# A first pass by single PSUM banks, maxima ahead of the turned tokens, and another opening and end, in a one-core attention and feed-forward kernel

## The reference

```python
xn = layernorm(x)                                   # last axis, 256
q = (xn @ wq + bq).reshape(b, s, 16, 16)            # 16 heads of 16
k = (xn @ wk + bk).reshape(b, s, 2, 16)             # 2 groups of keys and values
v = (xn @ wv + bv).reshape(b, s, 2, 16)
q, k = rotary(q) * 16 ** -0.5, rotary(k)
attn = softmax(q @ k.T * 16 ** -0.5)                # 1024 x 1024 for each batch and head
a = (attn @ v) @ wo + bo
hidden = silu(xn @ W1.T) * (xn @ W3.T)              # 1024 wide
f = fwht(hidden) @ W2.T                             # Walsh-Hadamard transform, scaled
return x + a + f
```

## Time and profile before

| what | us |
|---|---|
| median of three runs | 1079.11 (1078.23 to 1080.97) |
| the profiled execution, whole | 1075.6 |
| its span | 1073.8 |
| PE busy | 1014.3 |
| DVE busy | 771.2 |
| ACT busy | 707.5 |
| POOL busy | 347.2 |
| DVE's reductions of the first pass, L1295, 512 of them | 619.0 |
| DVE idle just before them | 235.7 |

### The profile page before, as it was taken

The page is one execution under the profiler, slowest core; times in us unless marked ns, Lnnn a source line. Parts: engine busy times, 40 slices in busy tenths (PEclk is TensorE's granted clock), DMA queues, the critical chain, the costliest instruction groups (busy, mean ns, idle before and its releaser), DMA issues.

```text
span 1073.8 us, 19578 instructions
## 1 busy us (share of the span) xinstructions
PE 1014.3 (94%) x7604; PEld 549.6 (51%) x7604; DVE 771.2 (72%) x934; ACT 707.5 (66%) x1336; POOL 347.2 (32%) x300
## 2 busy tenths in 40 slices
PE   4889999999999999999999999999999999999997
PEld 3554445545554555545554455545555454644454
DVE  5996688677776778767786777767776778776723
ACT  4256677657765777657776577667775678566873
POOL 5262722073312634054310735126320224012300
PEclk9998999999999999999999999999999999999999
DMA  8762155212052253402242250521123131510001
GB/s 234 177 172 75 53 137 104 74 57 86 17 117 78 76 136 66 100 21 84 64 103 74 97 126 18 117 64 51 51 62 71 33 83 33 111 32 6 12 8 50
DMA packets 64941, 84.03 MB, mean 78 GB/s; under 512 B 19960, under 2 KB 34168, under 8 KB 64848
## 3 DMA queue, kind: packets, MB, share of 16 engines
q1 hardware_dynamic: 63296, 80.74, 29.1%
q10 hardware_dynamic: 1552, 2.03, 0.7%
HBM read 54.97 MB, written 22.51 MB: 72 GB/s over the span
## 4 chain that ended last, share of the span: by engine, by line
PE 66%; DVE 17%; ACT 5%; issue 4%; DMA 4%; SPq 3%; POOL 2%; DVEq 0%; ACTq 0%; POOLq 0%
PE ps L1501 16%; PE ps L1558 14%; PE ps L1545 13%; DVE negpart L1295 11%; PE ps L1456 9%; PE ps L1513 8%; PE ps L1467 3%; DVE hid L1267 3%; PE ps L1434 3%; ACT work L1079 2%; DMA qk_parts<-hid 1%; DMA xn<-in_x 1%; SPq L776 1%; SPq L784 1%; DMA recip_rows<-dens 1%
## 5 line engine op out<-in xcount | busy, mean ns | idle before, releaser
L1295 DVE TENSOR_REDUCE negpart<-ps 128x2 f32<-128x1024 f32 x512 | 619.0, 1224 | 235.7 <-PE ps L1456 234.8
L1079 ACT ACTIVATE work<-ps 128x512 f32<-128x512 f32 x1024 | 560.0, 603 | 262.3 <-PE ps L1545 256.9
L1558 PE MATMUL ps<-work,vb 128*32 128x512 f32 x2048 | 274.6, 609 | 5.8 <-ACT osum L1090 5.0
L1545 PE MATMUL ps<-qh,kb 50*128 50x512 f32 x1024 | 265.1, 450 | 10.3 <-ACT work L1079 7.4
L1456 PE MATMUL ps<-kb,qh 48*128 48x512 f32 x1024 | 226.8, 433 | 9.6 <-DVE negpart L1295 5.3
L1545 PEld LDWEIGHTS ps<-qh,kb 50*128 50x128 f32 x1024 | 123.4, 185 | 212.3 <-ACT work L1079 159.0
L1501 PE MATMUL ps<-xf,w_p 64*128 64x512 f32 x1536 | 218.3, 400 | 7.4 <-DVE negpart L1295 1.4
L1501 PEld LDWEIGHTS ps<-xf,w_p 64*128 64x128 f32 x1536 | 143.6, 185 | 49.7 <-DVE hid L1267 16.3
L933 POOL TENSOR_TENSOR hid_p<-hid,hid_p 128x512 fp32r<-128x512 f32 x64 | 82.2, 1286 | 203.1 <-ACT hid_p L1068 203.1
L1456 PEld LDWEIGHTS ps<-kb,qh 48*128 48x128 f32 x1024 | 98.1, 185 | 82.7 <-DVE negpart L1295 48.4
L1513 PEld LDWEIGHTS ps<-w2t_p,hid_p 64*128 64x128 f32 x1536 | 107.7, 185 | 34.2 <-DVE negpart L1295 27.1
(11 more groups left out here) (125 smaller groups left out, 484.6 us busy)
## 6 DMA issues: line engine op xcount, KB each, us to landing
xf<-xn_parts SPq DMA_DIRECT2D x32, 512.0 KB, 8.5
qh<-qk_parts SPq DMA_DIRECT2D x192, 64.0 KB, 2.3
xn_parts<-xt SPq DMA_DIRECT2D x14, 512.0 KB, 3.5
qh<-mturned SPq DMA_DIRECT2D x256, 2.0 KB
y<-in_x SPq DMA_DIRECT2D x8, 512.0 KB, 4.8
attnt<-osum SPq DMA_DIRECT2D x124, 32.0 KB, 2.0
recips<-recip_rows SPq DMA_DIRECT2D x120, 32.0 KB, 1.8
xn<-in_x SPq DMA_DIRECT2D x7, 512.0 KB, 5.0
```

The lines of the kernel that those rows point to most:

```text
L1079: nc.scalar.activation(prob[(ITSTEPS * i + j) % NPROB][:, h, :], ps[:, 4 + u % 3, :], ACT.Exp, scale=SCALE).then_inc(exp_done, 1)
L1295: nc.vector.tensor_reduce(negpart[a][:, f, :, h, t, e], two(slot), AX.X, ALU.max, negate=True).then_inc(ring_free[slot], 1)
L1545: pe.matmul(ps[:, 4 + u % 3, :], kb[i % 2][rows, kt * P:(kt + 1) * P], qh[2 * a + f][rows, h, :], start=True, stop=True).then_inc(s2_done, 1)
L1558: m = pe.matmul(ps[VW * h:VW * (h + 1), 7, :], vb[b % 2][g][:, kt, :], prob[(ITSTEPS * i + j) % NPROB][:, h, :], start=(kt == 0), stop=(kt ...
```

## The change

- The first pass goes by single banks. `first(slot, 0)` issues the unit's half on the upper 64 rows into the slot's second bank, `first(slot, 1)` the other half into the first bank, and PE's order puts other work between them. DVE reduces each bank by itself: 1024 reductions of 128x512 instead of 512 of 128x1024. A half waits only for its own bank (the fourth field of `RING`), where the slot's last work was a unit too.
- PE's order in every kind of period is written anew, and in ACT's the place of `gate`, `linear`, `save_sums` and the projections' copies. WOo takes WO's order.
- SP: `place_maxima` and the reciprocals go ahead of `load_turned`.
- Opening: the first queries are copied from the rotated tiles straight into `qh` (`first_queries`, 24 transfers on SP's and ACT's queues), the turned tokens go from `xt` to `xf` (`copy_turned`); of the ten operations that rotate the second block's queries DVE keeps five, ACT has two and POOL three. EARLY is 3, so one UP piece more lies in iteration 0, in place of a period without own work.
- End: DN of iteration 7 begins a period earlier, the first half of the last WO is in its last period; the last sums are turned, divided and turned back on DVE, from PSUM, and multiplied with `wo_last`, a copy of the weights with zero rows.

The diff, cut to its core:

```diff
-EARLY = 4
-LATER = (4, 6, 8, 10)
-BEGIN = 8
+EARLY = 3
+LATER = (4, 6, 7, 8, 10)
+BEGIN = 12
 W2ALL = 32
-W2HEAD = 24
+W2HEAD = 20
...
+def down_at(i):
+
+    return range(12, 16) if i + 1 < NIT else range(11, 15)
...
+    if i + 1 == NIT and p == PERIODS - 1:
+        return ("WO", i, 0)
+    if p in down_at(i):
+        return ("DN", i, down_at(i).index(p))
...
-    def first(slot):
+    def first(slot, *halves):
         nonlocal unit
-        at = i + unit // (2 * UNITS)
-        if at < NIT:
-            piece(("S1", at, unit // UNITS % 2, unit % UNITS), 0, slot)
-        unit += 1
+        for n in halves:
+            at = i + unit // (2 * UNITS)
+            if at < NIT:
+                piece(("S1", at, unit // UNITS % 2, unit % UNITS), n, slot)
+            unit += n
...
         if kind in ("UP", "UPo"):
-            own(0, 1)
-            first(1)
+            own(0)
+            first(1, 0)
+            own(1)
+            first(1, 1)
             scores(0)
             sums_before()
+            first(1, 0)
             scores(1)
-            first(1)
-            own(2)
+            first(1, 1)
+            own(2, 3)
+            first(1, 0)
             scores(2)
-            own(3)
-            first(1)
+            first(1, 1)
             sums(i, 2 * p)
             scores(3)
-            first(1)
+            first(1, 0, 1)
...
+        elif kind in ("WO", "WOo"):
+            first(1, 0)
+            scores(0)
+            first(1, 1)
+            scores(1)
+            first(1, 0)
+            scores(2)
+            first(1, 1)
+            own(0, 1, 2, 3)
+            scores(3)
+            first(1, 0, 1)
+            sums_before()
+            first(0, 0, 1)
+            sums(i, 2 * p)
...
-def walk_closing(sums, piece, select):
+def walk_closing(sums, piece, last_values):
     sums(NIT - 1, ITSTEPS - 1)
-    select()
-    for half in range(QB):
-        for k in range(4):
-            piece(("WO", NIT - 1, half), k, 1 - half)
+    last_values()
...
+            at[entry] = (slot, full[slot], free[slot], free[slot] - (entry[0] == before[slot] == "S1"))
+            before[slot] = entry[0]
...
+            if m == 1:
+                return
...
+        def first_queries(queue, parts):
+
+
+            for part, n in parts:
+                queue.wait_ge(*rq(0, (6, 8, 9, 10)[part]))
+                for r in range(ROWT):
+                    for h in range(PAIRS):
+                        to = GRP * r + HD * n + HD // 2 * (part // 2)
+                        queue.dma_start(qh[0][to:to + HD // 2, h, :].bitcast(F32),
+                                        turning(0)[0][(0, 2, 3, 1)[part]][ROWT * h + r:P:NH, :]).then_inc(q_in[0], 16)
...
+            def copy_turned():
+
+                sp.wait_ge(*freed(("XT", 0)))
+                for n in range(2):
+                    for r in range(ROWT):
+                        for c in range(ROWT):
+                            sp.dma_start(xf[n][GRP * r:GRP * (r + 1), c:KC:ROWT, :].bitcast(F32),
+                                         xt[n][GRP * c:GRP * (c + 1), :, :].bitcast(F32)).then_inc(xf_in, 16)
...
-            store_turned(0)
             store_keys(sp, 0)
             swap_keys(1)
+            first_queries(sp, ((0, 0), (0, 2), (2, 0)))
+            store_keys(sp, 1)
+            copy_turned()
+            store_queries(1)
+            load_queries(0, 0, 1)
             store_queries(0)
-            store_keys(sp, 1)
-            load_queries(0, 0, 0)
-            load_turned(0)
-            store_queries(1)
             load_x(2)
-            load_queries(0, 0, 1)
+            place_maxima(0, 0, 0)
+            store_turned(1)
+            load_queries(0, 1, 0)
...
-                if after:
-                    load_turned(i + 1)
-                    load_queries(i + 1, 1, 0)
                 spread_recips(i, 0)
                 if after:
                     place_maxima(i + 1, 0, 0)
+                    load_queries(i + 1, 1, 0)
+                    load_turned(i + 1)
                     load_queries(i + 1, 1, 1)
...
+            a, b, t, u = turning(1)[0]
+            pool.wait_ge(*rq(1, RQ1))
+            nc.gpsimd.tensor_tensor(b, b, u, ALU.add).then_inc(q1_sum, 1)
+            pool.wait_ge(q1_hi, 1)
+            nc.gpsimd.tensor_tensor(t.bitcast(F32R), t, a, ALU.subtract).then_inc(q1_lo, 1)
+            pool.wait_ge(q1_hi, 2)
+            nc.gpsimd.tensor_tensor(b.bitcast(F32R), b, u, ALU.subtract).then_inc(q1_lo, 1)
...
+                for n, r in enumerate((1, 0)):
+                    dve.wait_ge(*filled(("S1", i, a, u), n + 1))
+                    nc.vector.tensor_reduce(negpart[a][:, f, r, h, t, e:e + 1], two(slot)[:, r, :], AX.X, ALU.max,
+                                            negate=True).then_inc(ring_free[slot], 1)
...
+                if k == 0 and RING[entry][3] > 0:
+                    pe.wait_ge(ring_free[slot], RING[entry][3])
+                if k == 1 and RING[entry][2] > RING[entry][3]:
...
+                    r = ROWT - 1 - k
+                    rows = slice(GRP * r, GRP * r + SROWS)
+                    m = pe.matmul(bank[:, r, :], qh[2 * q + f][rows, h, t * P:(t + 1) * P],
+                                  kb[i % 2][rows, e * 512:(e + 1) * 512], start=True, stop=True)
+                    done = True
...
+            def last_values():
+
+
+                pe.wait_ge(norm_done, 2 * NIT)
+                for k in range(BT):
+                    bank = ps[:, 2 + k, 0:D]
+                    pe.matmul(bank, attnt[0:GRP, 1, k * P:(k + 1) * P], wo_sb[0:GRP, NG - 1, :], start=True, stop=False)
+                pe.wait_ge(wo_last_in, 16 * QUAD)
+                for k in range(BT):
+                    pe.wait_ge(last_norm, k // 2 + 1)
+                    bank = ps[:, 2 + k, 0:D]
+                    m = pe.matmul(bank, last_attn[:, k * P:(k + 1) * P], wo_last, start=False, stop=True)
+                    if k % 2 == 1:
+                        m.then_inc(last_full, 1)
...
                     if kind == "UP":
                         exponentials(i, j, 0, 4)
                         hidden_before(i, p)
+                        gate(i, up_at(i).index(p))
                         exponentials(i, j, 4, 5)
-                        gate(i, up_at(i).index(p))
-                        exponentials(i, j, 5, 6)
                         linear(i, up_at(i).index(p))
-                        exponentials(i, j, 6, 8)
...
+            dve.wait_ge(pv_done, ITSTEPS * NIT)
+            for n, cols in enumerate(halves):
+                nc.vector.transpose(last_sums[:, cols], ps[:, 7, cols]).then_inc(last_turned, 1)
             for n in range(2):
-                cols = slice(n * 2 * P, (n + 1) * 2 * P)
-                dve.wait_ge(last_turned, 1)
-                nc.vector.reciprocal(last[GRP:P, cols], ps[GRP:P, 5, cols]).then_inc(last_recip, 1)
-                dve.wait_ge(last_turned, 2)
-                dve.wait_ge(last_recip, n + 2)
-                nc.vector.tensor_tensor(attnt[GRP:P, 1, cols], ps[GRP:P, 4, cols], last[GRP:P, cols],
-                                        ALU.mult).then_inc(last_norm, 1)
-            projected_sums(NIT - 1, 0)
+                dve.wait_ge(last_turned, n + 1)
+                nc.vector.reciprocal(shares[n], blocks[n][:, :, HD]).then_inc(last_step, 1)
             for n in range(2):
-                at = y[:, (NBLK - 1) % 2, 2 * n:2 * n + 2, :].rearrange("p t d -> p (t d)")
-                dve.wait_ge(*filled(("WO", NIT - 1, 1), n + 1))
-                nc.vector.tensor_tensor(at, at, two(0)[:, n, :], ALU.add).then_inc(ring_free[0], 1)
+                dve.wait_ge(last_step, n + 1)
```

More of the change, by code:

```diff
@@ L250, in walk_iteration @@
             scores(0)
-            first(1)
+            first(0, 0, 1)
+            first(1, 0)
             scores(1)
-            sums_before()
-            scores(2)
-            first(1)
-            own(0, 1)
-            sums(i, 2 * p)
-            first(1)
-            scores(3)
-            own(2, 3)
-            first(1)
-            extra()
-        elif kind == "WOo":
-            first(0)
+            first(1, 1)
+            scores(2)
+            own(0, 1, 2)
+            first(1, 0)
```

423 lines of the change are left out of this document (221 added, 202 removed).

## The result

The changed kernel takes 1063.61 us (median of four, 1059.54 to 1072.10) where the kernel before, run beside it, takes 1078.67: a ratio of 0.9853, 95% interval 0.9820 to 0.9886. A second measurement gave 0.9844 (0.9811 to 0.9877). So it is faster, by 15 us and not by the 44.5 forecast, and stands 1.6 above the range. The profiled execution took 1059.54 (span 1057.7).

The account below looks back on a forecast made before the run. PE and DVE were taken to wait for each other over both banks of slot 1. Terms -10 -9 -15 -10 +3 +3 -2.5 -4 sum to -44.5: 1031 from the profiled 1075.6, 1034.5 as median; range 1013 to 1062.

Parts of the forecast that it names:

- UP: UP periods in the loop: 7.4 us for 7.59, a gain of 10 in all (ends 0 and 29).
- DN: DN periods in the loop, 31 of them: 7.2 us against 7.45 on average, a gain of 9 (ends 0 and 14).
- Broken pairs: Rival, first pass: 543 same-row neighbours at 0.1 us each cost 54, kernel slower by 9 (1088 us); chance 0.07.
- Turning periods: Five stretches of 33.6 us: half units between score pairs fill PE's waits for ACT, 3.0 each, 15 gained (0 to 25).
- WOo: Four periods of about 11.3 us: WO's order, with copy and sums placed later, gains 2.5 each, 10 (0 to 14).
- Tokens: Iterations 6 and 7: turned tokens, issued later on SP's queue, come 0 to 5 us late twice, costing 3 (0 to 10).
- SP's queue otherwise: Maxima on SP's queue some 5 us earlier: no old stall to win back, though the shorter iteration would have met one.
- Opening: Opening: copies inside SBUF, first unit near 41, less lead, added UP piece and smoother start; 2.5 us gained in all.
- A smoother start: Opening: PE ran at 1.2 GHz from 78 to 89 after a wait; a smoother start wins 3 of about 5 us.
- End: Tail after the last sums' start: 9.2 us becomes 1.0 + 4.7, a gain of 4 (ends 0 and 5).
- DVE's load: DVE's 1024 short reductions: busy 703 us instead of 619, 84 more, on an engine judged not full.
- periods without own work: Seven periods left, near DVE's pace: eight short reductions cost 4.8 us for 4.6, 0.4 each with waits, +3.

Follow-up runs that it names:

- adjacent: Changed kernel with both halves of a unit issued together at the place of the second, banks still reduced singly: 1100.92 us, 1.0165 of the kernel before.
- lean_qk: Changed kernel with two instead of three matmuls per product in the projections of blocks 2 to 7: 1068.18 us, 0.9861 of the kernel before.
- tokens_undo: Changed kernel with SP's old order in every iteration, tokens and queries ahead of reciprocals and maxima: 1092.39 us, 1.0094 of the kernel before.
- before_gap: Kernel before with W2HEAD 20 instead of 24 and without the wait pacing the head of the weights' product: 1088.84 us, 1.0074 of the kernel before.
- head28: Changed kernel with W2HEAD 28 instead of 20, more of the weights' product ahead of the first unit: 1055.73 us, 0.9756 of the kernel before.
- best1: Changed kernel with W2HEAD 28 and, for iterations 6 and 7, tokens ahead of reciprocals and maxima: 1053.70 us, 0.9767 of the kernel before.
- best2: best1 with the second block's keys stored ahead of SP's last query copies and loaded on SP's queue, not ACT's: 1049.23 us, 0.9715 of the kernel before.

## Why the prediction was wrong, point by point

- **UP, -10 forecast**: right. 7.39 by the chain above, which has the product in it; 0.20 x 59 = 11.8.
- **DN, -9**: right, 7.22 for 7.2 forecast.
- **Broken pairs, the slower rival**: did not happen (adjacent).
- **Turning periods, -15**: the step's size failed. The four periods that took 33.6 take 32.4 now (33.2 in iteration 1): some 1.2 each and 5.8 in all. PE in time, their first matmul and the one behind them:

```profile
444.77 0.50 PE L1544 MATMUL ps<-kb,qh 48*128 48x512 f32 x1
...
477.13 0.86 PE L1587 MATMUL ps<-xf,w_p 64*128 64x512 f32 x6
```

  "PE's floor by the prices above is about 27.5" took pair prices from UP. Counted from one start to the next over this stretch, a score matmul takes 0.207 and a first-pass one 0.174, where a pair at 0.235 would be 0.118 each: 30.3 without a gap, and 2.1 of gaps. And lean_qk shows that less issue would have become waits for ACT, DVE and POOL.
- **WOo, -10**: mis-sized. From own(0) of the UP before to own(0) of the one behind is 16.4 for 17.2 in iteration 6 and for 18.8 in iteration 7: 0.7 and 2.4, of which 0.2 is the UP's. "Some 11.3" was the length of one of them; the other was 9.6. Those at period 0 took 9.3 up to UP's own(0) and take 8.3 if the wait for tokens is taken off: 1.0 each. That is 4.7 in all.
- **Tokens, +3**: the mechanism right, the size wrong. Waits of 3.37 and 4.18, in the two places named, and the clock behind them; iteration 7 with the end shows 6.0 between late (128.3) and in time (122.3), and with the 3.4 of iteration 6 that is some 9.5.
- **SP's queue otherwise, at nothing**: the new place of the maxima is worth 28.5 by tokens_undo. The prediction had seen that "the shorter iteration would have met one"; it did not price the clock behind such waits.
- **Opening, -2.5**: the step that failed worst. Up to the first score the sum held -2 (3 won at the first unit, 1 lost in the lead; its other two terms lie behind that score), and +10.1 came. "First unit near 41" rested on issues of 0.45; the copies took 0.76 each on SP and 0.84 for most on ACT, so that twelve on either queue took 9.2 and 9.3 and not 5.4, and the unit started at 43.54 for 43.61. The head shortened from 24 to 20 was not priced; with the queries no earlier, it made a wait of 3.86. "A smoother start would win some of about 5, I take 3" did not come: behind the first score the clock is at 0.50 again from 84 to 88 and from 96 to 100, and in the whole execution 18.6 us more of clock are lost, most of it ahead of the first score. before_gap (+8.3) and head28 (-7.9) put a price on the short head from both sides.
- **End, -4**: right. From the last sums' start to the last addition's end is 5.8 (1049.22 to 1055.04), for 9.8.
- **DVE's load**, in the argument and not in the sum: "84 more" busy time was forecast and 35.6 came. Reductions in a row overlap, 1024 of 685 ns being busy 659.1 and not 701. They still have 512 elements each, so the advice on tile size that the prediction sets against the edit is kept.

The books: the profiled execution is 16.1 shorter where the sum said 44.5, 28.4 missing. For the opening and iteration 0 the sum held 2.8 of gain (2.5 for the opening, 1.8 for UP and DN, less 1.5 for periods without own work), and 7.8 of loss came: 10.6 missing. For iterations 1 to 5 it held 27.6 (6.8 for UP, 5.8 for DN, 15 for turning), and 20.0 came: 7.6 missing, the turning periods' 9.2 less what UP did better. For iterations 6 and 7 with the end it held 14.2 (2.4 for UP, 2.3 for DN, 10 for WOo and 4 for the end, less 3 for tokens and some 1.5 for periods without own work), and 4.0 came: 10.2 missing, of which WOo is 5.3 and the tokens some 6.5, less a little that UP and DN did better. Open is how a wait and thin work share in the clock's fall in one execution: waits of 1.80 (best1) and 1.87 (before) stood ahead of a lead at 0.50 and of one at 1.00.

## What to carry to other kernels

Price a wait at the start of a dense stretch with the clock behind it: here 2 to 3 us more of idling cost 8. Split an operation to free a resource sooner only together with an order that uses the time between the parts: here the order without the split, and the split with its parts left together in that order, lost 11 and 7 us in the loop, where both together won 20. And when iterations shorten, look again at every transfer whose landing was just in time: the queue's order was worth 28.5 us here, more than the loops.

## What the runs showed of the hardware that was not expected

- Copies within SBUF of 8 rows, on two queues at once, were issued 0.64 to 0.84 us apart, where the reciprocals' loads from DRAM take 0.45.
- The clock fell from 1.00 to 0.50 without any wait above 0.2 us, when PE had only pairs of the first pass at DVE's pace (best2, at 51), and was 1.00 again by 62, after UP's matmuls had begun at 57.6.
- Some 543 neighbouring matmuls on the same rows of the array cost nothing that the trace shows: a half unit (507.41) joins the matmul beside it on the other rows, and the pairs still follow 0.23 apart.
- Six matmuls less in a stretch (lean_qk) made it 0.3 us shorter and not 1.5, and the clock fell in three of five such stretches.
